# Decoder layer on one Trainium2 core: v kept in its own order, filter matrices resident in SBUF, half of the block inversions moved into the recurrence

## What is computed

```python
for i in range(1, chunk):
    inv = inv.at[..., i, :].add(jnp.einsum('...j,...jk->...k', inv[..., i, :], inv))
inv = inv + jnp.eye(chunk, dtype=q.dtype)
u = inv @ v
w = inv @ kb
```

```python
local_long = causal_dwconv(v_in, fir_long.reshape(-1, fir_long.shape[-1])).reshape(B, L, H, dv)
local_short = causal_dwconv(v_in, fir_short.reshape(-1, fir_short.shape[-1])).reshape(B, L, H, dv)
```

## Time and profile before

| | us |
|---|---|
| median of 3 runs | 1317.78 |
| the profiled execution | 1323.56 |
| its span, first to last instruction | 1321.8 |
| first phase | 0 to 240.7 |
| second phase | 240.7 to 319.7 |
| third phase | from 319.7 |
| PE, DVE, ACT, POOL busy | 1119.9, 958.0, 898.0, 653.0 |
| mean granted clock of PE | 0.895 |

### The profile page before, as it was taken

The page is one execution under the profiler, slowest core; times in us unless marked ns, Lnnn a source line. Parts: engine busy times, 40 slices in busy tenths (PEclk is TensorE's granted clock), DMA queues, the critical chain, the costliest instruction groups (busy, mean ns, idle before and its releaser), DMA issues. The chain is left out here.

```text
span 1321.8 us, 28637 instructions
## 1 busy us (share of the span) xinstructions
PE 1119.9 (85%) x9251; PEld 820.2 (62%) x9251; DVE 958.0 (72%) x2132; ACT 898.0 (68%) x1743; POOL 653.0 (49%) x2200
## 2 busy tenths in 40 slices
PE   5998988783678799999999999999999888885756
PEld 4776766683566566766776776676677655443225
DVE  5999998698355657777877877777787566633985
ACT  5999998221344558787878878877887665453867
POOL 4777775563225544465465466547546543111007
PEclk9999998555557869999999999999999988897989
DMA  2443433893412434343433434343442342203106
GB/s 80 159 176 144 177 136 144 185 234 107 137 57 85 110 80 127 95 124 109 133 110 106 146 105 138 106 129 105 111 144 82 96 127 57 65 33 140 44 1 223
DMA packets 141779, 154.17 MB, mean 117 GB/s; under 512 B 48040, under 2 KB 106560, under 8 KB 141632
## 3 DMA queue, kind: packets, MB, share of 16 engines
q1 hardware_dynamic: 141632, 152.35, 38.4%
HBM read 93.32 MB, written 58.72 MB: 115 GB/s over the span
## 5 line engine op out<-in xcount | busy, mean ns | idle before, releaser
L2120 DVE TENSOR_REDUCE x_maxima<-x_psA 128x2 f32<-128x512 f32 x248 | 170.3, 687 | 96.2 <-PE x_psA L1448 93.7
L1704 ACT ACTIVATE x_PT<-x_psB 128x512 f32<-128x512 f32 x240 | 143.0, 596 | 56.5 <-PE x_psB L1472 52.1
L1711 ACT ACTIVATE x_psA<-x_mask_q 128x512 f32<-128x512 bf16 x239 | 142.4, 596 | 51.8 <-DVE x_maxima L2120 48.7
L297 DVE SCALAR_TENSOR_TENSOR a_conv<-a_ps_proj,taps,a_conv 128x253 f32<-128x253 f32 (+2 forms) x288 | 115.0, 471 | 8.4 <-ACT a_conv L364 8.4
L1448 PE MATMUL x_psA<-x_Ks,x_Qs 96*128 96x256 bf16 x496 | 99.5, 283 | 15.2 <-ACT x_psA L1711 14.7
L1469 PE MATMUL x_psB<-x_mask_k,x_ident_bf 128*128 128x512 bf16 x240 | 94.3, 393 | 13.0 <-ACT x_PT L1704 10.8
L533 PE MATMUL a_ps_proj<-a_hT,wqkv 128*128 128x256 f32 x384 | 93.2, 392 | 7.1 <-DVE a_conv L297 4.2
L1472 PE MATMUL x_psB<-x_Qs,x_Ks 98*128 98x256 bf16 x480 | 94.1, 277 | 0.0
L533 PEld LDWEIGHTS a_ps_proj<-a_hT,wqkv 128*128 128x128 f32 x384 | 71.5, 194 | 19.4 <-issue 6.6
L1864 POOL TENSOR_SCALAR x_parts_q<-x_rest 128x512 bf16<-128x512 f32 x16 | 23.9, 1494 | 116.3 <-DVE x_rest L2096 116.3
L1486 PE MATMUL x_psO<-x_PT,x_V 128*32 128x256 f32 x1024 | 72.0, 401 | 1.0 <-ACT x_PT L1704 1.0
(11 more groups left out here) (390 smaller groups left out, 3352.8 us busy)
## 6 DMA issues: line engine op xcount, KB each, us to landing
scratch_keypack<-a_keypack SPq DMA_DIRECT2D x16, 768.0 KB, 3.3
c_keypack<-scratch_keypack SPq DMA_DIRECT2D x16, 768.0 KB, 4.7
x_Ks<-scratch_k_parts SPq DMA_DIRECT2D x192, 64.0 KB, 2.2
b_matrix<-in_long_padded SPq DMA_DIRECT2D x16, 512.0 KB, 7.4
scratch_k_parts<-x_parts_k SPq DMA_DIRECT2D x32, 192.0 KB, 2.4
scratch_q_parts<-x_parts_q SPq DMA_DIRECT2D x32, 192.0 KB, 2.3
x_Qs<-scratch_q_parts SPq DMA_DIRECT2D x32, 192.0 KB, 3.0
a_x_in<-in_x SPq DMA_DIRECT2D x16, 256.0 KB, 2.7
```

Of the source, the lines that this page charges most:

```text
L297: nc.vector.scalar_tensor_tensor(acc, ps_proj[PROJ_BANK[p]][:, c, 0:L - j], taps[:, p, c, TAPS - 1 - j:TAPS - j], acc, ALU.mult, ALU.add). ...
L1704: nc.scalar.activation(PT[:, k % (2 * GROUP)], bank_B(b, k)[0], ACT.Exp, scale=XD ** -0.5).then_inc(pexp_ready, 1)
L1711: nc.scalar.activation(psA[:].rearrange("p t q -> p (t q)"), mask_q[:, k % 2].rearrange("p s k -> p (s k)"), ACT.Copy).then_inc(mask_writt ...
L2120: nc.vector.tensor_reduce(maxima[:, t, 2 * pair:2 * pair + 2], bank_A(b, k)[0], AX.X, ALU.max).then_inc(maxed, 1)
```

## The change

- v is kept in its order. The flips and their copies are gone; ACT copies v straight into `v_windows`, the store of v reads from there, and two SBUF-to-SBUF DMAs in each turn (`win`) make the shifted half window. The flip is in the filter matrices.
- All filter matrices stay in SBUF (`matrix`, 128 partitions x 256 channels x 64). At the start one HBM-to-HBM DMA writes 16 copies of each channel's 192 padded taps (256 x 16 x 192 x 4 bytes, 3.1 MB); in each turn of the first phase one DMA (`taps`) places 16 partitions by 128 channels by 64 taps (512 KB in pieces of 256 bytes). `taps` waits for that copy, and stands ahead of `ld_x` in SP's order.
- The first phase has another order, with 6 stages in place of 5 behind the first. `stat` is at stage 1 and stands before `conv_k` (4) on DVE; two weight loads fewer are waited for.
- The second phase has no matrix loads. A channel takes one matmul of 64 moving columns in place of two of 32; the two channels of a pair write the two halves of the partitions. The result is stored in 2 stages of 4 DMAs, in pieces of 256 bytes (512 before). The three constant loads and five loads for the third phase are issued at once.
- Of the four groups of inversions only 0 and 1 stay in the second phase, each on its own on DVE; POOL takes no chain there, and sets the upper triangle and the diagonal with small memsets in place of the mask. Groups 2 and 3 go, together in one instruction, to DVE in the third phase: new steps `inv0` right behind `tt` in `C_ORDER`, `inv1` behind `att0`, `inv2` behind `att1`. They turn in at turn 0, do j = 1 to 3 and 4 to 16 in turn 0, 17 to 19 and 20 to 23 in turn 1, 24 to 26 and 27 to 30 in turn 2, and turn back at turn 3. POOL sets their upper parts (126 memsets) ahead of `rv` of sample 0. They use memory of `x_PT`, which is first written at turn 5. Waits for their end are added where sample 8 begins and at the first `eB`.

```diff
+A_ORDER = [(6, "dk"), (5, "proj_v"), (4, "gbias"), (3, "st_hT"), (4, "tail"), (4, "silu_q"), (4, "tanh"),
+           (4, "silu_k"), (4, "norm"), (6, "short2"), (6, "short_t"), (5, "ktok"), (4, "tap_v"), (5, "gsc"),
+           (6, "st_k"), (1, "taps"), (6, "win"), (6, "st_p"), (3, "tap_k"), (5, "stok"), (4, "sq0"), (5, "tok0"),
+           (4, "sq1"), (1, "stat"), (3, "turn_h"), (6, "st_s"), (5, "tok1"), (5, "conv_v"), (6, "ksT"),
+           (4, "conv_k"), (0, "ld_x"), (4, "proj_q"), (5, "norms"), (2, "hTc"), (4, "silu_v"), (4, "ks"),
+           (5, "tok2"), (5, "vtok"), (4, "conv_q"), (6, "diag"), (5, "short1"), (3, "gate"), (5, "kpk"),
+           (3, "tap_q"), (0, "rstd"), (6, "st_v"), (1, "xn"), (3, "proj_k"), (4, "stap")]
+
+
+W_LOADS = 16 * 9
+FIR_COLS = P + HB
+COPIES = 16
...
+                    sp.dma_start(dram["v_tok"][b], keep["v_windows"][:, 1, :, b]).then_inc(v_stored, 16)
+                elif op == "taps":
+                    row, half = b // FC, b % FC
+                    sp.wait_ge(taps_copied, 16)
+                    taps_of = bass.AP(dram["taps_copies"].tensor, half * P * COPIES * FIR_COLS + P - 1 - row,
+                                      [[FIR_COLS - STEP, COPIES], [COPIES * FIR_COLS, P], [1, HB]])
+                    sp.dma_start(keep["matrix"][row:P:STEP, half * P:half * P + P], taps_of).then_inc(taps_placed, 16)
+                elif op == "win":
+                    sp.wait_ge(v_tok_ready, b + 1)
+                    sp.dma_start(keep["v_windows"][HB:P, 0, :, b], keep["v_windows"][0:HB, 1, :, b]).then_inc(window_set, 16)
+                    sp.dma_start(keep["v_windows"][0:HB, 0, 1, b], keep["v_windows"][HB:P, 1, 0, b]).then_inc(window_set, 16)
...
-            sp.dma_start(flip[:], dram["flip"]).then_inc(w_loaded, 16)
-            sp.dma_start(half_flip[:], dram["half_flip"]).then_inc(w_loaded, 16)
+
+            sp.dma_start(dram["taps_copies"], bass.AP(dram["long_padded"].tensor, 0, [[FIR_COLS, D], [0, COPIES], [1, FIR_COLS]])).then_inc(taps_copied, 16)
...
-                elif op == "fA":
-                    act.wait_ge(v_flipped, b + 1)
-                    nc.scalar.activation(keep["v_windows"][:, 1, :, b], ps_tok[2][:], ACT.Copy).then_inc(flip_kept, 1)
-                elif op == "fB":
-                    act.wait_ge(half_flipped, b + 1)
-                    act.wait_ge(window_zero, 1)
-                    nc.scalar.activation(keep["v_windows"][0:HB, 0, :, b], ps_tok[2][0:HB], ACT.Copy)
-                    nc.scalar.activation(keep["v_windows"][HB:P, 0, 1, b], ps_tok[2][HB:P, 1], ACT.Copy).then_inc(half_kept, 1)
+                    nc.scalar.activation(keep["v_windows"][:, 1, :, b], ps_tok[2][:], ACT.Copy).then_inc(v_tok_ready, 1)
...
-                elif op == "flipA":
-                    pe.wait_ge(v_tok_ready, b + 1)
-                    after(b, (half_kept, 0, 1), (v_tok_ready, 0, 1), (flip_kept, -1, 1))
-                    nc.tensor.matmul(ps_tok[2][:].rearrange("p t c -> p (t c)"), flip[:], v_tok[:].rearrange("p t c -> p (t c)"),
-                                     start=True, stop=True).then_inc(v_flipped, 1)
...
-CG = 16
-GROUPS = D // CG
-DEPTH = 4
+EARLY_GROUPS = 2
+CHAIN_STEPS = 2 * (CH - 2)
+
+
+def substitution(M, product, j):
+
+    n, rows = M.shape[1], CH - 1 - j
+    return (product[:, :, 0:rows * j].rearrange("p q (i j) -> p q i j", j=j), M[:, :, j + 1:CH, 0:j],
+            M[:, :, j + 1:CH, j:j + 1].broadcast_to([P, n, rows, j]), M[:, :, j:j + 1, 0:j].broadcast_to([P, n, rows, j]))
+
+
+CG = 8
+GROUPS = P // CG
+DEPTH = 8
 EARLY_AT = 4
...
-                sp.dma_start(matrix[n][:], src).then_inc(loaded[n], 16)
...
+            for stage in range(2):
+                sp.wait_ge(kept, (stage + 1) * (GROUPS // 2))
+                for half in range(FC):
+                    for part in range(2):
+                        at = slice(half * P + stage * HB, half * P + stage * HB + HB)
+                        sp.dma_start(dram["long_tok"][part * HB:part * HB + HB, :, :, at].rearrange("p t b c -> p (t b) c"),
+                                     keep["long"][half * HB:half * HB + HB, part, :, stage * HB:stage * HB + HB]).then_inc(long_stored, 16)
...
-                for c in range(CG):
-
-                    for part in range(2):
-                        last = nc.tensor.matmul(psum[n][part * HB:part * HB + HB, c].rearrange("p t b -> p (t b)"),
-                                                matrix[n][:, c], keep["v_windows"][:, part, :, :, group * CG + c].rearrange("p t b -> p (t b)"),
+                for i in range(CG):
+                    for half in range(FC):
+                        c = half * P + group * CG + i
+                        last = nc.tensor.matmul(psum[n][half * HB:half * HB + HB, i], keep["matrix"][:, c],
+                                                keep["v_windows"][:, :, :, :, c].rearrange("p a t b -> p (a t b)"),
                                                 start=True, stop=True, skip_group_check=True)
...
+            for q in range(EARLY_GROUPS):
+                pool.wait_ge(M_turned, q + 1)
+                for i in range(CH):
+                    nc.gpsimd.memset(M[q][:, i, i:i + 1], 1.0)
+                for i in range(CH - 1):
+                    last = nc.gpsimd.memset(M[q][:, i, i + 1:CH], 0.0)
+                last.then_inc(upper_cleared, 1)
 
         @block.vector
         def _(dve):
-            for q in (NQ - 1, 0, 1, 2):
-                nc.vector.transpose(M[:, q].rearrange("p i j -> p (i j)"), keep["diag"][:, q * CH:(q + 1) * CH].rearrange("p s c -> p c s")).then_inc(M_turned, 1)
-            dve.wait_ge(M_turned, NQ)
+            for q in range(EARLY_GROUPS):
+                if q > 0:
+                    dve.wait_ge(M_turned, q)
...
+                steps = [substitution(M[q][:].unsqueeze(1) if q == 0 else M[q].unsqueeze(1), products[q].unsqueeze(1), j) for q in range(EARLY_GROUPS)]
+                for q, (out, below, left, row) in enumerate(steps):
+                    if j > 1:
+                        dve.wait_ge(chain[q], 2 * j - 2)
+                    nc.vector.tensor_tensor(out, left, row, ALU.mult).then_inc(chain[q], 1)
+                for q, (out, below, left, row) in enumerate(steps):
+                    dve.wait_ge(chain[q], 2 * j - 1)
+                    nc.vector.tensor_tensor(below, below, out, ALU.add).then_inc(chain[q], 1)
...
-            for step, q, n in ((chain_pair, 0, 2), (chain_single, 2, 1), (chain_pool, 3, 1)):
-                dve.wait_ge(step, CHAIN_STEPS)
-                nc.vector.tensor_tensor(M[:, q:q + n], M[:, q:q + n], lower[:].unsqueeze(1).broadcast_to([P, n, CH, CH]),
-                                        ALU.mult).then_inc(M_masked, 1)
-            dve.wait_ge(M_masked, 3)
-            nc.vector.memset(M[:].rearrange("p q i j -> p q (i j)")[:, :, 0:CH * CH:CH + 1], 1.0).then_inc(M_masked, 1)
-            dve.wait_ge(M_masked, 4)
-            for q in range(NQ):
-                at = slice(q * CH, (q + 1) * CH)
-                nc.vector.transpose(keep["X32"][:, at].rearrange("p s i -> p i s"), M[:, q])
+            dve.wait_ge(upper_cleared, EARLY_GROUPS)
+            for n, q in enumerate(reversed(range(EARLY_GROUPS))):
+                dve.wait_ge(chain[q], CHAIN_STEPS)
+                if n > 0:
+                    dve.wait_ge(X_turned, n)
+                nc.vector.transpose(keep["X32"][:, q * CH:(q + 1) * CH].rearrange("p s i -> p i s"),
...
+        ALL_STEPS = LATE_GROUPS + CHAIN_STEPS + LATE_GROUPS
+        LATE_STEPS = {(0, 1): (1, 4), (0, 2): (4, 17), (1, 1): (17, 20), (1, 2): (20, 24), (2, 1): (24, 27), (2, 2): (27, CH - 1)}
...
+        M = PT[:, 4:8].rearrange("p g t n -> p (g t n)").rearrange("p (q i j) -> p q i j", q=LATE_GROUPS, j=CH)
+        product = PT[:, 2].rearrange("p t n -> p (t n)").rearrange("p (q n) -> p q n", q=LATE_GROUPS)
...
+                elif (b, op) == (0, "inv1"):
+                    for q in range(LATE_GROUPS):
+                        pool.wait_ge(inverse_step, q + 1)
+                        for i in range(CH):
+                            nc.gpsimd.memset(M[:, q, i, i:i + 1], 1.0)
+                        for i in range(CH - 1):
+                            last = nc.gpsimd.memset(M[:, q, i, i + 1:CH], 0.0)
+                        last.then_inc(upper_cleared, 1)
...
+                elif op[:3] == "inv":
+                    if (b, op) == (0, "inv0"):
+                        for q in range(LATE_GROUPS):
+                            at = (EARLY_GROUPS + q) * CH
+                            nc.vector.transpose(M[:, q].rearrange("p i j -> p (i j)"),
+                                                keep["X32"][:, at:at + CH].rearrange("p s c -> p c s")).then_inc(inverse_step, 1)
+                    elif (b, int(op[3])) in LATE_STEPS:
+                        dve.wait_ge(inverse_step, LATE_GROUPS)
+                        for j in range(*LATE_STEPS[b, int(op[3])]):
```

(26 more changed lines are left out.)

151 lines of the change are left out of this document (46 added, 105 removed), and 4 rows, old and new, of the table C_ORDER.

## The result

The changed kernel takes **1362.3 us** (median of 4 runs, 1360.1 to 1367.3), the kernel before 1317.5 (4 runs, 1314.0 to 1319.6): ratio 1.035, 95% interval 1.032 to 1.038, slower by 45 us. Forecast were 1298 us and a range of 1284 to 1316. The profiled execution took 1360.1 us, its span 1358.3, against 1321.8 before.

The account below looks back on a forecast made before the run. DVE was taken to bound the first two phases, a PE-ACT-DVE chain the third's first turns. Terms: first phase +4, second -39, third +15, together -20 from the median 1317.8, giving 1298 us; range 1284 to 1316.

Parts of the forecast that it names:

- First phase, the turns: First phase, 15 turns: with the flips gone DVE stops waiting, pitch 12.3 us instead of 13.1; -11.5 us.
- the bound on the other side: First phase, turns: the worst case allowed was no gain, the pitch staying at 13.1 us.
- Rival 3: First phase: the new order only moves the wait, the turn stays at 13.1; 12 us more, 1310 us; chance 0.12.
- The start: First phase up to the first L306: x waits behind HBM copy and taps, 47.3 us against 30.3; +17 us.
- The tail: End of the first phase, behind the last L306: the flip between the last `ks` and `diag` goes; -1.9 us.
- Second phase, DVE: Second phase: DVE's turning in and back, inversion chain, constants, starts and waits take 38.3 us.
- Second phase, PE: Second phase, filter: 512 records are 256 pairs at 107 ns, at half clock; 27.3 us.
- Stores: Second phase, after the filter: last copy and issue 0.9, 2 MB in 256-byte pieces 9.2, landing 2 us.
- Rival 2: Second phase: 256-byte store pieces double in price, the phase ends at 53 us, not 40; 1311 us; chance 0.15.
- the sign I gave for it: Second phase: an end past 45 us with SP waiting for the long store would mean small store pieces cost double.
- Third phase: Third phase, first turns: the two late inversion groups on DVE delay r1 by 10 us, then +3, 1, 1; +15 us.

Follow-up runs that it names:

- no_taps: The changed kernel without the HBM copy and the 16 loads of taps, GpSimd filling the filter matrices with zeros; 1327.5 us.
- contig: The changed kernel with the filter's moving operand read from 64 adjacent columns of v_windows; second phase 37.9 us, a pair 58 ns at full clock.

## Why the prediction was wrong

**First phase, the turns: here it failed.** The step reads "Both now have 10.5 us or less in a turn against DVE's 12.3, so DVE should stop waiting." The loads were right (DVE has 99.9 / 130 x 16.1 = 12.4 us a turn), the conclusion was not: the turn grew by 1.9 us on average where it was to shrink by 0.8. An engine with the most work sets the pace only if no loop of waits is longer, and the prediction looks at the waits between engines, not at one through SP and a landing. The order put `st_p` late in a burst that begins with `hTc`, and its waiter, `silu_q`, at the head of ACT's next turn: 3.7 + 5.3 + 6.8 = 15.8 us. Opening it with a third pack gave back 19.8 us of the phase, SP in the makers' order 25.6. I had written of SP that its issues "lie in a queue that mostly waits for ACT"; that wait is what gathers them into the burst. And "the bound on the other side is nothing (13.1 stays)" was no bound: 40 us of the miss of 56 are here. Rival 3 named the mechanism ("The new order only moves the wait") and kept it at before's pace, 12 us, and 0.12.

**The start: right.** 49.2 against 47.3; the copy lands at 21.05 as forecast, and `no_taps` shows that copy and taps make 17.4 of the 18.9.

**The tail**: the flip is gone and the tail is no shorter, +0.2 for -1.9; what holds it there wasn't tried.

**Second phase, DVE: right.** 37.6 in `contig` for 38.3. In the run after it is 41.7: turning in took 0.9 longer, and at one place the chain waits 3.0 us for a constant that ACT makes behind the copy of the seventh filter group, so the slow filter reaches DVE too:

```profile
307.38 0.15 DVE L717 TENSOR_SCALAR c_temp<-c_temp 128x1 f32<-128x1 f32 x1 [2.98 <-ACT c_static L678]
```

**Second phase, PE: the term was mis-sized**, 27.3 us forecast and 37.6 measured. I took the pair from L1292 for its shape and its clock, and that row reads its moving operand contiguously. The clock was not the forecast's 0.5 but 0.86 in the phase, and with this stride that gave nothing back. The Trainium skill (SBUF — State Buffer, Door 1: The DMA port swizzle) says that consecutive accesses to the same line of 16 bytes run at full bandwidth and that each access to a new line pays a penalty; I hadn't weighed it. The runs agree, 58 against 123 and 146 ns; for the difference of 1024 and 1032 bytes it has nothing.

**Stores: 12.1 became 14.1.** Rival 2's doubling didn't come (+2 us), and that the phase ended past 45 with SP at the store, the sign I gave for it, came from the late filter. The Trainium skill (DMA: Bandwidth & Descriptors, Specifications) wants at least 512 bytes for line rate; 174 against 203 GB/s agrees in direction, and is far from the doubling that I drew from it.

**Third phase: right**, +15.4 for +15, r1 at 30.0 for 30.4; that the sum is so near is in part luck. Up to the `tt` of sample 3 the loss is 17.3 (94.9 - 77.6), of which the prediction had 10 at r1 and 4 in turns 1 and 2; behind it 1.9 come back, where equal kernels differ by 3.6. The steps alone are worth 17.1.

By the measured terms: 47.8 - 26.8 + 15.4 = 36.4, where the span grew by 36.5.

## What to carry to other kernels

Before crediting a removed wait, follow each buffer round: its maker, the place of its store in the queue, the landing, the next writer. If the store's place in a burst plus its landing plus the path back is longer than the busiest engine's turn, that is the turn. Order an in-order queue by when sources are made, not by stages. And take a matmul's time from a row with the same stride, not only the same shape.
